# A gated attention layer whose prologue works by contraction steps: x, context and k's weight in pieces, q's weight ahead of v's, and batch 0's deviations by Ln, Exp and one Newton step

## The chip, the cores and the metric

The kernel runs on one core of one Trainium2 chip. The metric is device time in microseconds (us): of the kernel before, three runs gave 1958.17 to 1960.98 with a median of 1960.36. The engines are TensorE (PE; its weight loads are PEld), VectorE (DVE), ScalarE (ACT), GpSimd (POOL) and SyncE, whose queue (SPq) issues all transfers.

## What is computed

For 16 batches of 512 tokens with 512 channels, all float32: a gated cross-attention of the normalised x over a context, and a gated feed-forward of the result:

```python
m, v = mean(x), var(x); n = (x - m) / sqrt(v + 1e-5)        # layernorm, no weights
q = n @ Wq.T + bq;  k = ctx @ Wk.T + bk;  v = ctx @ Wv.T + bv    # 16 heads of 32
attn = softmax(mask_and_causal(q @ k.T * 32**-0.5)) @ v
x = x + tanh(g_xattn) * (attn @ Wo.T + bo)
y = layernorm(x); yp = y shifted by one token
r = sigmoid((mu_r*y + (1-mu_r)*yp) @ W_r.T);  kk = (mu_k*y + (1-mu_k)*yp) @ W_k.T
out = x + tanh(g_ffn) * r * (relu(kk)**2 @ W_v.T)
```

## The kernel before

Every engine's program is written out by hand and every engine runs its own in order; the engines meet at semaphores. One of 16 batches is a tile of 4 x 128 tokens by 4 x 128 channels. The channels are the contraction of the projections, so a projection of 128 output rows has four steps k = 0..3.

**Exact products.** A float32 operand is split in a high part (rounded to the matmul's fp32r, a CAST on ScalarE) and a low part (original minus high, a subtraction on VectorE). `exact_product` makes three 128x512 matmuls for each step k (L41 high by high, L42 and L43 the mixed ones). So each weight (wq, wk, wv, wo), the context c (kept transposed) and the transposed x all cost a ScalarE cast and a VectorE subtraction before TensorE can use them. `split_weights` (L642 on ScalarE, L1007 on VectorE) does that for a weight as a whole, 128x2048; for batch 0 the context is also done as a whole (L829, L1156).

**x.** VectorE takes statistics of four token blocks (L931, L938), GpSimd turns variance to 1/sqrt in `invert_deviations` (L470 to L486: an integer seed and three Newton steps, 16 dependent instructions), ScalarE applies it (`apply_layernorm`, L566), TensorE transposes each block with the identity (L1362, four 128x128), ScalarE casts (`high_part_x`, L573), VectorE subtracts (`low_part_x`, L942).

**q and k.** A projected group of four heads leaves its PSUM bank by ScalarE (high part, L582 for q, L591 for k), then VectorE (low part, L947, L953), and then by six DMAs that stack the parts into `q_stack` and `k_stack` (`stack_q`, `stack_k`, L305, L314), with rows for the mask, whose constant part GpSimd sets to 1.0 first (L532, `stacks_set`). v goes to SBUF by `copy_v` (L599).

**Slots.** After a prologue, 259 slots follow, one for each (batch, head): scores of head i (L1236), their row extrema by VectorE (L964), and for head i - 3 the probabilities (L1260), their exponent (L619), causal masking and partial sums on GpSimd (L440 to L457), every fourth slot the values (L1280 to L1290). The table `WORK` says which steps of the projections of this batch and the next lie in which slot. PSUM has two banks for projections and one for values; `BANK` and `BEFORE` say which tile uses which and whose reader must have ended (`free_bank`). From about 1340 us on the feed-forward follows.

**The prologue**, the part that the change touches, makes in this order on TensorE: k0 (four steps), x blocks 0 and 1, v0, x blocks 2 and 3, v1, q0, two steps of q1; then slot 0, whose scores wait for `q_stacked` and `k_stacked`. ScalarE begins with the gates (Tanh) and a table load for Exp and Ln:

```python
act.wait_ge(gate_loaded, 16)
act.wait_ge(pool_const, 5)
nc.scalar.copy(ident_parts[:], ident[:]).then_inc(ident_ready, 1)
nc.scalar.activation(gate[:], gate[:], ACT.Tanh).then_inc(gate_ready, 1)
```

SyncE's queue issues x as 1 MB, two gates, c, wk, wv, wq, bias columns, mu, mask, wo, bo (L292 and L396 to L410), and then waits for `mask_scaled`, stores the mask and stacks.

## Time and profile before

| | |
|---|---|
| median of 3 runs | 1960.36 us (1958.17 to 1960.98) |
| the profiled execution | 1958.57 us, its span 1956.8 us |
| granted TensorE clock, mean | 0.99 of 2.4 GHz |
| PE busy | 1898.7 us, 97% of the span |
| PEld busy | 1471.8 us, 75% |
| DVE busy | 1339.0 us, 68% |
| ACT busy | 1088.0 us, 56% |
| POOL busy | 1210.6 us, 62% |
| DMA moved | 229.66 MB, mean 117 GB/s |

The profile is of one execution. In the page's strip of 40 slices PE is busy at 4 tenths in the first slice and at 8 in the second, and at 9 in nearly all others. Busy time is of instructions in flight, so a PE that is busy throughout can still run at either level of its clock; the granted clock (PEclk) tells which.

### The profile page before, as it was taken

Reading aid. Unit: us, or ns where it says so; the run is one execution under the profiler, and the core shown is the slowest. Engines: PE = TensorE matmul, PEld = TensorE weight load, DVE = VectorE, ACT = ScalarE, POOL = GpSimd, SP = SyncE. Lnnn points to the kernel's source line nnn. Section 1 sums busy time; section 2 is a strip of 40 time slices with the busy share of each in tenths; the row PEclk is TensorE's granted clock in tenths of the full one; section 3 lists DMA queues with packets and bytes.
Section 4 is the critical chain, followed back from the end, with each engine's and each line's share of the span. In section 5 each row is a group of like instructions: output and inputs, shape, how many; then the busy total and the mean of one; then the engine's idle time right before and its main releaser. Section 6 shows DMA issues by size and latency. Waiting matters only on the chain.

```text
span 1956.8 us, 35230 instructions
## 1 busy us (share of the span) xinstructions
PE 1898.7 (97%) x11136; PEld 1471.8 (75%) x11136; DVE 1339.0 (68%) x3528; ACT 1088.0 (56%) x2059; POOL 1210.6 (62%) x2001
## 2 busy tenths in 40 slices
PE   4899999999999999999999999998989999999999
PEld 3677777777777777777777777776768888888887
DVE  4767767777676777777677677777566665756654
ACT  4555555555555555555555555555565666656562
POOL 4577767777777777767777677777633333434331
PEclk9999999999999999999999999998999999999999
DMA  6454554645545445554545446454223223232321
GB/s 190 104 126 117 140 128 108 163 109 126 126 122 156 118 121 122 136 147 104 143 117 137 122 114 164 112 139 122 72 102 108 87 91 104 75 108 76 108 65 65
DMA packets 128695, 229.66 MB, mean 117 GB/s; under 512 B 18656, under 2 KB 20704, under 8 KB 127616
## 3 DMA queue, kind: packets, MB, share of 16 engines
q1 hardware_dynamic: 128512, 227.43, 43.6%
q8 instruction: 90, 1.47, 0.3%
q14 instruction: 93, 0.76, 0.1%
HBM read 92.06 MB, written 33.59 MB: 64 GB/s over the span
## 4 chain that ended last, share of the span: by engine, by line
PE 75%; DVE 10%; POOL 6%; issue 5%; ACT 3%; DMA 1%; SPq 0%; ACTq 0%; POOLq 0%; DVEq 0%
PE proj_ps L41 12%; PE proj_ps L42 11%; PE proj_ps L43 11%; PE value_ps L1280 7%; PE score_ps L1236 6%; PE prob_ps L1260 5%; PE score_ps L41 3%; PE score_ps L42 3%; PE score_ps L43 3%; DVE score_ps L964 2%; PE sum_ps L1290 2%; DVE split_max L974 2%; PE sum_ps L43 1%; PE sum_ps L42 1%; PE value_ps L42 1%
## 5 line engine op out<-in xcount | busy, mean ns | idle before, releaser
L964 DVE CUSTOM_DVE_ANT_0 score_ps<-score_ps,causal 128x128 f32<-128x128 f32 (+3 forms) x1024 | 487.6, 505 | 284.6 <-PE score_ps L1236 282.9
L619 ACT ACTIVATE probs<-prob_ps 128x512 f32<-128x512 f32 (+1 forms) x768 | 394.3, 527 | 313.8 <-PE prob_ps L1260 179.1
L1236 PE MATMUL score_ps<-k_stack,q_stack 97*128 97x128 f32 (+3 forms) x1024 | 319.2, 353 | 9.0 <-DVE least L964 3.7
L1260 PE MATMUL prob_ps<-q_stack,k_stack 100*128 100x512 f32 (+3 forms) x1024 | 282.5, 317 | 6.1 <-ACT probs L619 4.6
L451 POOL TENSOR_TENSOR prob_sum<-probs 128x384 f32<-128x384 f32 x256 | 259.4, 1013 | 0.0
L1236 PEld LDWEIGHTS score_ps<-k_stack,q_stack 97*128 97x128 f32 x1024 | 188.6, 190 | 83.3 <-issue 30.7
L500 POOL TENSOR_TENSOR kact<-square,kact 128x512 fp32r<-128x512 f32 x64 | 83.9, 1322 | 235.3 <-ACT kact L695 235.3
L454 POOL TENSOR_TENSOR prob_sum<-prob_sum,probs 128x256 f32<-128x256 f32 x256 | 193.9, 758 | 37.3 <-POOL prob_sum L451 0.9
L1260 PEld LDWEIGHTS prob_ps<-q_stack,k_stack 100*128 100x128 f32 x1024 | 192.8, 192 | 28.9 <-issue 6.9
L440 POOL TENSOR_SCALAR_AFFINE_SELECT probs<-probs 128x256 f32<-128x256 f32 x256 | 104.8, 409 | 177.2 <-ACT probs L619 177.2
L444 POOL TENSOR_SCALAR_AFFINE_SELECT probs<-probs 128x256 f32<-128x256 f32 x256 | 106.9, 418 | 103.3 <-ACT probs L619 103.3
L1280 PE MATMUL value_ps<-probs,v 128*32 128x512 f32 (+3 forms) x2048 | 165.6, 442 | 0.1
L964 DVE DVE_READ_ACCUMULATOR2_ANT least<- 128x1 f32 x1024 | 144.4, 141 | 0.0
L1031 DVE TENSOR_TENSOR square<-square 128x512 f32<-128x512 f32 x64 | 45.5, 712 | 139.0 <-ACT square L687 138.9
L457 POOL TENSOR_TENSOR prob_sum<-prob_sum,probs 128x128 f32<-128x128 f32 x256 | 120.5, 471 | 20.1
L1020 DVE SCALAR_TENSOR_TENSOR tiles<-xT_room_high,mu,tiles 128x512 f32<-128x512 f32 x128 | 94.8, 760 | 49.5 <-ACT tiles L667 47.0
L41 PE MATMUL proj_ps<-cT_high,wk_high 128*128 128x512 f32 x256 | 102.4, 400 | 18.0 <-DVE wk_low L1007 18.0
L606 ACT COPY max_rows<-sum_ps 16x128 f32<-16x128 f32 x128 | 32.5, 254 | 152.8 <-PE sum_ps L1245 152.8
L41 PE MATMUL proj_ps<-mix_k_high,ffn_wk_high 128*128 128x512 f32 x256 | 104.3, 408 | 4.8 <-DVE mix_k_low L1026 3.6
L41 PE MATMUL proj_ps<-wo_high,attn_high 128*128 128x512 f32 x256 | 103.0, 402 | 2.1 <-DVE attn_low L995 1.3
L41 PE MATMUL proj_ps<-xT_high,wq_high 128*128 128x512 f32 x256 | 102.1, 399 | 1.6 <-DVE staged L947 1.6
L41 PE MATMUL proj_ps<-wv_high,cT_high 128*128 128x512 f32 x256 | 101.6, 397 | 1.0 <-DVE xT_low L942 1.0
(145 smaller groups left out, 4873.7 us busy)
## 6 DMA issues: line engine op xcount, KB each, us to landing
k_stack<-staged SPq DMA_DIRECT2D x384, 128.0 KB
q_stack<-staged SPq DMA_DIRECT2D x384, 128.0 KB, 3.1
tiles<-in_x SPq DMA_DIRECT2D x16, 1024.0 KB, 5.6
x_io<-in_x SPq DMA_DIRECT2D x16, 1024.0 KB, 7.9
x<-x_io SPq DMA_DIRECT2D x64, 256.0 KB, 3.1
res<-x SPq DMA_DIRECT2D x64, 256.0 KB, 3.7
out_x<-res SPq DMA_DIRECT2D x64, 256.0 KB, 2.0
tiles<-in_ctxT SPq DMA_DIRECT2D x60, 256.0 KB, 4.4
```

Source lines behind the costliest of these rows:

```text
L41: nc.tensor.matmul(out, s_high, m_high, start=first and n == steps[0], stop=False)
L42: nc.tensor.matmul(out, s_high, m_low, start=False, stop=False)
L43: done = nc.tensor.matmul(out, s_low, m_high, start=False, stop=last and n == steps[-1])
L444: nc.gpsimd.affine_select(out=pair, in_=pair, compare_op=ALU.is_ge, fill=0.0, base=0, pattern=[[0, 2], [1, P]], channel_multiplier=-1).the ...
L451: nc.gpsimd.tensor_tensor(total, here[:, P:S], here[:, PT_AT[1]:PT_AT[1] + LATE], ALU.add).then_inc(summed, 1)
L454: nc.gpsimd.tensor_tensor(total[:, P:LATE], total[:, P:LATE], here[:, PT_AT[2]:PT_AT[2] + 2 * P], ALU.add).then_inc(summed, 1)
L457: nc.gpsimd.tensor_tensor(total[:, 2 * P:LATE], total[:, 2 * P:LATE], here[:, PT_AT[3]:PT_AT[3] + P], ALU.add).then_inc(summed, 1)
L619: nc.scalar.activation(probs[:, u % RING, lo:hi], prob_ps[(3 * u + c) % 2][:, 0:hi - lo], ACT.Exp, scale=SCALE).then_inc(exp_done, 1)
L964: nc.vector.tensor_tensor_reduce(out=here, in0=here, in1=causal[:, LATE - P * t:S], scale=-1.0, scalar=3e38, op0=ALU.add, op1=ALU.min, acc ...
L1236: last = nc.tensor.matmul(here[:, at:at + P * (t + 1)], q_stack[n][0:MASK_ROW + 1, j, P * t:P * t + P], k_stack[n][0:MASK_ROW + 1, j, 0:P ...
L1260: last = nc.tensor.matmul(here[:, at:at + width], k_stack[n][0:ROWS, j, P * k:P * k + P], q_stack[n][0:ROWS, j, P * k:S], start=True, stop ...
L1280: nc.tensor.matmul(value_ps[DH * j:DH * j + DH, P * k:S], v[:, value_block(b, g), k, at:at + DH], probs[:, (HG * G + j) % RING, PT_AT[k]:P ...
```

## The change

It touches the first part of every engine's program. Transfers: the mask goes first, x comes as four blocks of 256 KB with a semaphore each, then c and wk by contraction step in turn (eight times 256 KB), then wq, wv, the columns, the mask's store, wo, and only then gates, mu and bo. ScalarE and VectorE split c and the four weights by step. Batch 0's deviations are made by Ln and Exp(-0.5 ln) on ScalarE and one Newton step of four small instructions on VectorE; GpSimd's 16 instructions for batch 0 go. GpSimd does the mask and the constant rows of the stacks at once, and the wait for those rows before the first scores is taken by TensorE. TensorE makes k0 in two halves with the transposes between and after them, then q0, then v0 and v1, and q1's two steps now wait for v0's copy. The Tanh of both gates stands behind the weights' casts on ScalarE, with a table load on either side of it. The diff, cut to its core:

```diff
-        FIRST = {"k0": None, "x0": None, "v0": ("x0", 0), "x2": ("v0", 0), "q1": ("q0", 0)}
+        FIRST = {"k0": None, "x0": None}
...
-            load_x(0)
+            sp.dma_start(x_io[0:B, 0, :].bitcast(I32), mask).then_inc(mask_loaded, 16)
+            for m in range(T):
+                sp.dma_start(tiles[:, m, :], x[0, P * m:P * m + P]).then_inc(x_first_loaded[m], 16)
+            for k in range(K):
+                sp.dma_start(c_raw[:, k, :], ctxT[0, P * k:P * k + P]).then_inc(c_first_loaded[k], 16)
+                sp.dma_start(w_raw["k"][:, k, :], wkT[:, k, :]).then_inc(wk_first_loaded[k], 16)
+            sp.dma_start(w_raw["q"], wqT).then_inc(w_loaded["q"], 16)
+            sp.dma_start(w_raw["v"], wvT).then_inc(w_loaded["v"], 16)
+            for n, col in enumerate((bq, bk, bv)):
+                sp.dma_start(columns[:, n, :], col).then_inc(columns_loaded, 16)
+            sp.wait_ge(mask_scaled, 1)
+            sp.dma_start(mask_bias, x_io[0:B, 1, :]).then_inc(mask_stored, 16)
+            sp.dma_start(w_raw["o"], woT).then_inc(w_loaded["o"], 16)
             sp.dma_start(gate[:], g_xattn.partition_broadcast(P)).then_inc(gate_loaded, 16)
             sp.dma_start(ffn_gate[:, 0:1], g_ffn.partition_broadcast(P)).then_inc(ffn_gate_loaded, 16)
-            sp.dma_start(c_raw, ctxT[0].rearrange("(k p) s -> p k s", p=P)).then_inc(c_raw_loaded, 16)
-            sp.dma_start(w_raw["k"], wkT).then_inc(w_loaded["k"], 16)
-            sp.dma_start(w_raw["v"], wvT).then_inc(w_loaded["v"], 16)
-            sp.dma_start(w_raw["q"], wqT).then_inc(w_loaded["q"], 16)
-            for n, col in enumerate((bq, bk, bv)):
-                sp.dma_start(columns[:, n, :], col).then_inc(columns_loaded, 16)
             for n, col in enumerate((mu_k, mu_r)):
                 sp.dma_start(mu[:, n, :], col).then_inc(mu_loaded, 16)
-            sp.dma_start(x_io[0:B, 0, :].bitcast(I32), mask).then_inc(mask_loaded, 16)
-            sp.dma_start(w_raw["o"], woT).then_inc(w_loaded["o"], 16)
             sp.dma_start(bo_gated[:], bo.partition_broadcast(P)).then_inc(bo_loaded, 16)
-            sp.wait_ge(mask_scaled, 1)
-            sp.dma_start(mask_bias, x_io[0:B, 1, :]).then_inc(mask_stored, 16)
...
-            invert_deviations(0)
-            pool.wait_ge(ln_step, NORM_STEPS)
-            for n, rows in enumerate(q_stack + k_stack):
-                nc.gpsimd.memset(rows[MASK_ROW:P].bitcast(F32), 1.0).then_inc(stacks_set, 1)
-                pool.wait_ge(stacks_set, n + 1)
...
             pool.wait_ge(mask_loaded, 16)
             nc.gpsimd.tensor_scalar(x_io[0:B, 1, :], x_io[0:B, 0, :].bitcast(I32), 0, MASKED, ALU.is_equal,
                                     ALU.mult).then_inc(mask_scaled, 1)
+            pool.wait_ge(pool_const, 5)
+            pool.wait_ge(mask_scaled, 1)
+            for n, rows in enumerate((k_stack[0], q_stack[0], k_stack[1], q_stack[1])):
+                nc.gpsimd.memset(rows[MASK_ROW:P].bitcast(F32), 1.0).then_inc(stacks_set, 1)
+                pool.wait_ge(stacks_set, n + 1)
...
+            def split_first_c(k):
+                act.wait_ge(c_first_loaded[k], 16)
+                nc.scalar.copy(cT[0][:, k, :], c_raw[:, k, :]).then_inc(c_high, 1)
+
+            def split_weights(name, k):
+                if name == "k":
+                    act.wait_ge(wk_first_loaded[k], 16)
+                else:
+                    act.wait_ge(w_loaded[name], 16)
+                nc.scalar.copy(w[name][0][:, k, :], w_raw[name][:, k, :]).then_inc(w_high[name], 1)
...
-            act.wait_ge(gate_loaded, 16)
+            nc.scalar.preload_act_table_set("natural_log_exp_and_others")
+            split_first_c(0)
+            act.wait_ge(variance_ready, 1)
+            nc.scalar.activation(newton[:, 1, :], newton[:, 2, :], ACT.Ln).then_inc(variance_logged, 1)
+            act.wait_ge(variance_logged, 1)
+            nc.scalar.activation(newton[:, 1, :], newton[:, 1, :], ACT.Exp, scale=-0.5).then_inc(seed_ready, 1)
...
             act.wait_ge(pool_const, 5)
             nc.scalar.copy(ident_parts[:], ident[:]).then_inc(ident_ready, 1)
+            act.wait_ge(gate_loaded, 16)
             nc.scalar.activation(gate[:], gate[:], ACT.Tanh).then_inc(gate_ready, 1)
             act.wait_ge(ffn_gate_loaded, 16)
             nc.scalar.activation(ffn_gate[:, 1:2], ffn_gate[:, 0:1], ACT.Tanh).then_inc(ffn_gate_tanh, 1)
             nc.scalar.preload_act_table_set("natural_log_exp_and_others")
...
-            dve.wait_ge(c_high, K)
-            nc.vector.tensor_tensor(cT[1][:], c_raw, cT[0][:].bitcast(F32), ALU.subtract).then_inc(c_low, K)
-            split_weights(0, "k")
-            split_weights(1, "v")
+            power, guess, variance, shift = (newton[:, n, :] for n in range(4))
+            dve.wait_ge(ln_stats, T)
+            nc.vector.tensor_scalar(variance, moments[:, :, 1], LN_EPS, None, ALU.add).then_inc(variance_ready, 1)
+            low_part_first_c(0)
+            dve.wait_ge(seed_ready, 1)
+            nc.vector.tensor_tensor(power, guess, guess, ALU.mult).then_inc(seed_step, 1)
+            dve.wait_ge(seed_step, 1)
+            nc.vector.scalar_tensor_tensor(out=power, in0=power, scalar=-0.5, in1=variance, op0=ALU.mult, op1=ALU.mult
+                                           ).then_inc(seed_step, 1)
+            dve.wait_ge(seed_step, 2)
+            nc.vector.scalar_tensor_tensor(out=guess, in0=power, scalar=1.5, in1=guess, op0=ALU.add, op1=ALU.mult
+                                           ).then_inc(seed_step, 1)
+            dve.wait_ge(seed_step, 3)
+            nc.vector.scalar_tensor_tensor(out=shift, in0=moments[:, :, 0], scalar=-1.0, in1=guess, op0=ALU.mult, op1=ALU.mult
+                                           ).then_inc(ln_step, NORM_STEPS)
+            split_weights("k", 0)
+            low_part_first_c(1)
+            split_weights("k", 1)
+            low_part_first_c(2)
+            split_weights("k", 2)
             low_part_x(0, 0)
-            low_part_x(0, 1)
+            low_part_first_c(3)
+            split_weights("k", 3)
+            for m in range(1, T):
+                low_part_x(0, m)
+            for k in range(K):
+                split_weights("q", k)
             low_part_k(0, 0)
-            split_weights(2, "q")
-            low_part_x(0, 2)
-            low_part_x(0, 3)
+            split_weights("v", 0)
+            split_weights("v", 1)
             low_part_q(0, 0)
+            split_weights("v", 2)
+            split_weights("v", 3)
...
+                if c == 0 and u in (0, HG):
+                    pe.wait_ge(stacks_set, (2, 4)[G])
...
-            pe.wait_ge(ident_ready, 1)
-            for k in range(K):
+            for k in range(2):
                 project_k(0, 0, k)
             transpose_x(0, 0)
             transpose_x(0, 1)
-            for k in range(K):
-                project_v(0, 0, k)
+            for k in range(2, K):
+                project_k(0, 0, k)
             transpose_x(0, 2)
             transpose_x(0, 3)
             for k in range(K):
-                project_v(0, 1, k)
-            for k in range(K):
                 project_q(0, 0, k)
+            for m in range(2):
+                for k in range(K):
+                    project_v(0, m, k)
+            pe.wait_ge(ident_ready, 1)
             for k in range(2):
```

On ScalarE, before: its first twelve instructions. `probs` is the room in which c, wk and wq arrive, `attn_room` that of wv and wo, `tiles` is x, `staged` are q's and k's parts on their way to the stacks.

```order
L823 ACT_TABLE_LOAD [waits pool_const]
L823 CAST ident_parts<-ident 128x128 [waits gate_loaded]
L824 ACTIVATE gate<-gate 128x1
L826 ACTIVATE ffn_gate<-ffn_gate 128x1 [waits ffn_gate_loaded]
L827 ACT_TABLE_LOAD
L829 CAST cT_high<-probs 128x2048 [waits c_raw_loaded]
L642 CAST wk_high<-probs 128x2048 [waits wk_loaded]
L566 ACTIVATE tiles<-tiles,newton 128x512 [waits ln_step] x4
L642 CAST wv_high<-attn_room_high 128x2048 [waits wv_loaded]
L573 CAST xT_high<-proj_ps 128x4x128 [waits xt_done]
L573 CAST xT_high<-value_ps 128x4x128 [waits xt_done]
L591 ACTIVATE staged<-proj_ps,columns 128x512 [waits k_done,columns_loaded]
```

And now, from the casts of wq to the copies of v:

```order
L654 CAST wq_high<-probs 128x512 [waits wq_loaded] x4
L596 ACTIVATE staged<-proj_ps,columns 128x512 [waits k_done,columns_loaded]
L654 CAST wv_high<-attn_room_high 128x512 [waits wv_loaded] x2
L587 ACTIVATE staged<-proj_ps,columns 128x512 [waits q_done]
L654 CAST wv_high<-attn_room_high 128x512 [waits wv_loaded] x2
L865 CAST ident_parts<-ident 128x128 [waits pool_const]
L867 ACT_TABLE_LOAD
L867 ACTIVATE gate<-gate 128x1 [waits gate_loaded]
L869 ACTIVATE ffn_gate<-ffn_gate 128x1 [waits ffn_gate_loaded]
L870 ACT_TABLE_LOAD
L604 COPY v<-proj_ps 128x2x256 [waits v_done] x2
```

The two table loads around Tanh stood ahead of all casts and now stand behind those of wq and wv, directly ahead of v's copies; q's high part (L587) now comes between v's casts.

On TensorE, before: from k0's last step to the first scores. A step of a projection is three rows and a transposed block two; here the first row of each stands, and of the steps that only repeat, none.

```order
L41 MATMUL proj_ps<-cT_high,wk_high 128x512 [waits w_low,c_low]
L1362 MATMUL proj_ps<-ident,tiles 128x128 [waits ln_applied]
L1362 MATMUL value_ps<-ident,tiles 128x128 [waits ln_applied]
L41 MATMUL proj_ps<-wv_high,cT_high 128x512 [waits w_low,c_low,xt_low]
...
L1362 MATMUL proj_ps<-ident,tiles 128x128 [waits ln_applied,v_copied]
L1362 MATMUL value_ps<-ident,tiles 128x128 [waits ln_applied,xt_low]
L41 MATMUL proj_ps<-wv_high,cT_high 128x512 [waits k_low]
...
L41 MATMUL proj_ps<-xT_high,wq_high 128x512 [waits w_low,xt_low]
...
L41 MATMUL proj_ps<-xT_high,wq_high 128x512 [waits q_low]
...
L1236 MATMUL score_ps<-k_stack,q_stack 128x128 [waits k_stacked0_0,q_stacked0_0]
```

And now, from k0's second step on:

```order
L41 MATMUL proj_ps<-cT_high,wk_high 128x512 [waits wk_low,c_low]
L1427 MATMUL proj_ps<-ident,tiles 128x128 [waits ln_applied]
L1427 MATMUL value_ps<-ident,tiles 128x128 [waits ln_applied]
L41 MATMUL proj_ps<-cT_high,wk_high 128x512 [waits wk_low,c_low]
...
L1427 MATMUL proj_ps<-ident,tiles 128x128 [waits ln_applied,xt_low]
L1427 MATMUL value_ps<-ident,tiles 128x128 [waits ln_applied,xt_low]
L41 MATMUL proj_ps<-xT_high,wq_high 128x512 [waits wq_low,xt_low]
...
L41 MATMUL proj_ps<-wv_high,cT_high 128x512 [waits wv_low,c_low,q_low]
...
L41 MATMUL proj_ps<-wv_high,cT_high 128x512 [waits k_low]
...
L41 MATMUL proj_ps<-xT_high,wq_high 128x512 [waits v_copied,ident_ready]
...
L1298 MATMUL score_ps<-k_stack,q_stack 128x128 [waits stacks_set,k_stacked0_0,q_stacked0_0]
```

q0 moved ahead of v0 and v1, so that 24 matmuls of v and six of q1 now stand between the end of q0 and the first scores, where six of q1 stood; q1 waits for v's copy and no longer for q0's low part.

## Rows read from the trace of the kernel before

**Rows 1.** Windows by stage: window, length, busy us of each engine, PEclk, DMA share, GB/s

```profile
18.00:40.70 22.70, 16.64 (x70) 12.65 (x70) 8.57 (x8) 10.51 (x12) 10.62 (x7) 1.00 0.40 106
40.70:48.50 7.80, 7.01 (x19) 5.59 (x20) 3.68 (x15) 0.69 (x1) 0.00 (x0) 0.56 0.83 205
48.50:100.00 51.50, 46.51 (x253) 33.15 (x256) 37.19 (x121) 26.36 (x53) 30.00 (x62) 0.90 0.51 109
100.00:1340.00 1240.00, 1231.85 (x7981) 932.54 (x7974) 906.80 (x2740) 681.38 (x1368) 923.72 (x1550) 1.00 0.52 128
```

**Rows 2.** Chain of waits, 0 to 50 us: start, us, what

```profile
2.79 10.81 DMA probs<-in_wkT
...
15.55 2.30 DVE wk_low L1007
17.99 0.77 PE proj_ps L41
...
25.98 0.23 PE proj_ps L41
...
34.65 0.70 ACT staged L582
...
36.15 0.57 SPq L305
...
44.66 0.43 PE proj_ps L41
```

**Rows 3.** Windows of the first transfers

```profile
5.50:7.00 1.50, 0.00 (x0) 0.00 (x0) 0.97 (x2) 0.00 (x0) 0.00 (x0) 1.00 0.04 2
...
8.50:11.00 2.50, 0.00 (x0) 0.00 (x0) 0.38 (x5) 1.27 (x1) 1.42 (x8) 1.00 1.09 435
```

**Rows 4.** Timeline 0 to 20 us: start, us, engine, line, operation [idle before <-releaser]

```profile
0.80 0.45 SPq L292 DMA_DIRECT2D tiles<-in_x  x1
...
6.03 2.47 DVE L931 BATCH_NORM_STATS2 stats<-tiles 128x6 f32<-128x512 f32 x4 [6.03 <-DMA tiles<-in_x]
...
7.14 0.30 ACT L823 CAST ident_parts<-ident 128x128 fp32r<-128x128 f32 x1 [3.55 <-DMA gate<-in_g_xattn]
7.35 0.20 ACT L824 ACTIVATE gate<-gate 128x1 f32<-128x1 f32 x1
...
8.49 1.28 ACT L827 ACT_TABLE_LOAD   x1
8.54 0.38 DVE L938 BATCH_NORM_AGGREGATE moments<-stats 128x2 f32<-128x6 f32 x4
...
11.19 1.90 ACT L829 CAST cT_high<-probs 128x2048 fp32r<-128x2048 f32 x1 [1.42 <-DMA probs<-in_ctxT]
...
15.61 2.93 ACT L566 ACTIVATE tiles<-tiles,newton 128x512 f32<-128x512 f32 x4
15.63 3.66 POOL L532 MEMSET q_stack<- 32x2048 f32 x2
```

**Rows 5.** Answers by source line: duration ns min/median/max, first and last start

```profile
L296 SPq DMA_DIRECT2D tiles<-in_ctxT x60: 327/442/2009, 92.9 to 1260.6; - x60
...
DMA to landing us min/median/max: 2.9/4.4/6.5
...
L612 ACT CAST cT_high<-tiles x60: 608/627/641, 95.9 to 1271.0; 128x512 fp32r<-128x512 f32 x60
L573 ACT CAST xT_high<-proj_ps x32: 557/585/589, 23.0 to 1259.7; 128x512 fp32r<-128x512 f32 x32
L974 DVE TENSOR_TENSOR split_max<-least,split_max x128: 166/169/1208, 49.7 to 1378.6; 128x8 fp32r<-128x8 f32 x128
```

**Rows 6.** Timeline of TensorE: the first scores and the first values

```profile
40.71 0.67 PE L1236 MATMUL score_ps<-k_stack,q_stack 97*128 97x128 f32 x3 [2.87 <-DMA q_stack<-staged]
...
76.97 1.06 PE L1280 MATMUL value_ps<-probs,v 128*32 128x512 f32 x8
```

**Rows 7.** Window of a later stretch at the lower clock

```profile
74.00:76.00 2.00, 2.00 (x7) 1.60 (x6) 1.59 (x4) 1.13 (x4) 1.86 (x4) 0.54 1.10 160
```

More of the change, by code:

```diff
@@ L147, in gated_layer @@
         sum_ps = psum("sum_ps")
-        w_loaded = {n: sem(f"w{n}_loaded") for n in "qkvo"}
-        w_high, w_low = sem("w_high"), sem("w_low")
+        w_loaded = {n: sem(f"w{n}_loaded") for n in "qvo"}
+        w_high, w_low = ({n: sem(f"w{n}_{part}") for n in "qkvo"} for part in ("high", "low"))
         ffn_loaded = {n: sem(f"ffn_w{n}_loaded") for n in "krv"}
@@ L162, in gated_layer @@
         xt_done, xt_high, xt_low = sem("xt_done"), sem("xt_high"), sem("xt_low")
-        c_raw_loaded = sem("c_raw_loaded")
+        variance_ready, variance_logged, seed_ready, seed_step = (sem(f"first_{n}") for n in ("variance", "logged", "seed", "step"))
+        x_first_loaded = [sem(f"x_first_loaded{m}") for m in range(T)]
+        c_first_loaded = [sem(f"c_first_loaded{k}") for k in range(K)]
+        wk_first_loaded = [sem(f"wk_first_loaded{k}") for k in range(K)]
         c_loaded = [sem(f"c_loaded{k}") for k in range(K)]
@@ L928, in layernorm_stats @@
             def layernorm_stats(b, m):
-                dve.wait_ge(x_loaded, 16 * (b + 1))
+                if b == 0:
+                    dve.wait_ge(x_first_loaded[m], 16)
+                else:
+                    dve.wait_ge(x_loaded, 16 * b)
                 wait(dve, ln_stats, T * b)
@@ L1117, in fourth @@
                     layernorm_stats(b + 1, 2)
[L1118 to L1119 removed]
+                if i in (1, 2):
+                    for k in range(2):
+                        split_weights("o", 2 * (i - 1) + k)
                 if i == N - 9:
@@ L1326, in project_v @@
                     pe.wait_ge(c_low, K * (b + 1))
-                    pe.wait_ge(w_low, 2)
+                if b == 0 and m == 0:
+                    pe.wait_ge(w_low["v"], k + 1)
                 last = exact_product(nc, bank(f"v{m}")[:], lambda k: [part[:, k, P * m:P * m + P] for part in cT],
@@ L1468, in _ @@
             pe.wait_ge(pool_const, 5)
-            pe.wait_ge(ident_ready, 1)
-            for k in range(K):
+            for k in range(2):
                 project_k(0, 0, k)
@@ L1478, in _ @@
             for k in range(K):
-                project_v(0, 1, k)
-            for k in range(K):
                 project_q(0, 0, k)
+            for m in range(2):
+                for k in range(K):
+                    project_v(0, m, k)
+            pe.wait_ge(ident_ready, 1)
             for k in range(2):
```

65 lines of the change are left out of this document (38 added, 27 removed).

## The prediction

> **What bounds the kernel now.** I read the stages first [rows 1]. From 100 to 1340 us TensorE is in flight for 1231.85 of 1240 us at full clock, and no edit is there. The change is about what comes before: TensorE's first matmul starts at 17.99 us [rows 2], from 18 to 40.7 us it is busy for 16.6 of 22.7, and only then do the 259 slots begin. Every later slot is placed relative to the first scores and not to the clock on the wall, so what counts is when slot 0 starts and how well the first slots run. Bounds of the rest (97% TensorE) don't move.
>
> The chain of waits [rows 2] names what sets 40.71 us. At its head one transfer, wk, in flight from 2.79 to 13.6 us; then its cast (until 15.55) and its subtraction (2.30), then the first matmul. At its tail: q0 has ended at 34.6, ScalarE's high part (0.70) and VectorE's low part last until 36.15, 1.5 us in all; there the DMAs for q's stack begin, and the first scores, which wait for them, start at 40.71 [rows 6]. So q is last, and 4.56 us pass between its first DMA and the scores. The windows of the transfers [rows 3] show that from 8.5 us on the queue moves 435 GB/s (0.60 us for 256 KB, 2.4 us for 1 MB) and that from 5.5 to 7.0 us it moves nothing, although c had been issued long before. The two gate DMAs lie between x and c there.
>
> **The change, step by step.**
>
> *Transfers.* x was issued at 0.80 us and VectorE could begin at 6.03 [rows 4]. A mask DMA of half a microsecond now stands ahead, so the last block of x lands at some 6.3 us, the first at 4.5. A 256 KB issue takes the queue 0.44 us [rows 5], less than the 0.60 us that its bytes need, so bytes set the pace. If the hole goes with the gates, c's first step lands at 6.9 and each of the seven pieces after it 0.62 us later: wk complete at 11.3 (before: 13.6), wq at 13.7, wv at 16.2. If the hole stays, all of these are 2 us later. I take that it goes, because c's bytes start only behind the gates' landing; the other end stays in the range. The Trainium skill ("DMA: Bandwidth & Descriptors", Rules for kernel authors) asks for at least 1 MiB per DMA for full bandwidth, which speaks against eight pieces of 256 KB. No row here shows pieces alone: the four of load_c land in 4.4 us in the middle [rows 5], beside stack DMAs.
>
> *Deviations.* Before, GpSimd's chain let the normalising start at 15.61 [rows 4]. Now: last statistics at 7.1, aggregation 0.38, one small VectorE instruction, Ln and Exp at about 0.2 each (Tanh of the gate took that [rows 4]), four small VectorE instructions at 0.17 to 0.21 each (one of that size stands in [rows 5]), plus the crossings: done at 9.0. First matmul: wk's first low part is behind that on VectorE, 0.7 us for a quarter of 2.30 and its fixed part, so about 9.8 instead of 17.99.
>
> *The new bound of the prologue is ScalarE, in order.* From c's first step (7.0) to the cast of wq's last step it has 12 casts (0.627 each alone, some 0.54 back to back [rows 5]) = 6.5; Ln and Exp 0.4; four normalisings 2.93 [rows 4]; four x casts of 0.585, overlapped 0.5 [rows 5] = 2.0; sum 11.8, so 18.8 without a wait. Waits I find when I lay the programs side by side: 1.2 us for the transpose of x block 0 (it stands behind two steps of k0, which run at the lower clock), 1 to 2 us for block 2, whose bank waits for VectorE's low part. wq's last cast then ends between 20.6 and 21.9, its subtraction 0.7 later, the step of q0 another 1 to 1.3 later. q0 ends at **24.1** (22.6 at best, 25.9 if TensorE is at 1.2 GHz throughout). Before: 34.6. Splitting a 2048-wide cast in four costs 4 x 0.54 against 1.90, 0.25 us each; that is in the sum.
>
> *q's low part.* 1.5 us as before, giving 25.6 instead of 36.12. VectorE has two subtractions of wv ahead of it, done by 24.7, so they hide. k's stack DMAs end at 26.2 (SyncE's queue, k's low part at 23.6 plus 1.9 and 0.7), so q's are issued at 26.2 and land at 30.8.
>
> *What is late next.* Between q0 and the scores TensorE now has v0, v1 and two steps of q1, 30 matmuls. v0 shares q0's bank and starts at 25.7. Pitch is 0.23 at full clock and 0.43 at half [rows 2]: 6.9 us at full, so 32.5; with all q0 and the first of v at half clock, 34.3. I take **33.3**. The DMAs (30.8) hide behind them. Before 40.71: gain **7.4** (8.2 to 6.4, and 2 less if the hole stays).
>
> *The clock in the first slots.* Before, TensorE had waited 2.87 us for q's stack [rows 6]; the granted clock then fell to half, mean 0.56 from 40.7 to 48.5 us [rows 1], the matmuls of a projection there at 0.43 pitch. A mean of 0.56 is 0.88 of 7.8 us, nearly 7, at half clock, of which some 6.4 in matmuls, worth up to 3.2. Now TensorE goes from q1 straight to the scores, so the cause is gone. VectorE's extrema and the stack DMAs hold part of it back: I take **2.2** (0 to 3.2).
>
> *Edits at nothing.* GpSimd's fills (3.66 for two [rows 4]) now end before 14 us and are wanted at 33; without that cover they would cost 7 us. The gate's wait (3.55 us [rows 4]) hid behind c, for which ScalarE waited another 1.42 us; going alone it would bring nothing. The Tanh group (0.3 + 1.28 + 0.4 + 1.28 = 3.3 us) now stands ahead of v0's copy, which q1's steps wait for: it ends at 29.1 to 29.7, and v1 keeps TensorE until 31.1. Gates landing: behind wo, at some 22, wanted at 27. wo's split: in idle ScalarE time of slot 0; VectorE takes it in two slots instead of one, which lets k1's low part through about 1 us earlier.
>
> One rule speaks against that group's new place. Both table loads show 1.28 us (one in [rows 4]), and what follows each in the trace waited for something else anyway, so no drain can be read. The Trainium skill ("ScalarE: Activation LUTs", What ACT_TABLE_LOAD costs) gives a drain of about 1.38 us with every switch.
>
> **Sum.** 7.4 + 2.2 = 9.6 us. The profiled execution took 1958.57 (span 1956.8 and 1.8 around it): 1949.0. It lies 1.8 below the median of the runs, near their lower end, so I put the new median at **1949.5**.
>
> **Rivals.**
>
> 1. *The hole stays or the pieces are slow.* For: 1.5 us without bytes [rows 3] may belong to the switch from x to c and not to the gates. Against: the queue never pauses between the other 1 MB loads. Price: c at 9.0, all of ScalarE's chain 2 us later, and matmuls at half clock: first scores 34.6 to 36.4, gain 4.3 to 6.1, plus up to 2.2 from the clock; about 1953.5. Chance 0.20.
> 2. *A table switch holds ScalarE longer than its 1.28 us*, by one more of the same length or so each. v0's copy then ends at 31.9 to 32.5, TensorE waits at q1 for some 1.3 us: 1950.8. By the skill's drain it would be the same within 0.2. Chance 0.07.
> 3. *More comes back.* The later drops to half clock (one is in [rows 7]) are what makes 0.90 of 48.5 to 100 us [rows 1]: 0.2 x 51.5 = 10 us at half clock, at 0.46 us each (1 - 0.23/0.43) some 4 us of matmuls; they follow short waits for GpSimd and x, and a differently paced start could miss them: 1945. Chance 0.07.
> 4. *No gain.* The dense start earns a new drop: 48.5 to 100 us already runs at 0.90 of the clock with 5 us of idle [rows 1]. Each microsecond at half clock costs 0.46. If the early slots spend some 17 us more at half clock, 8 of the 9.6 are gone: 1957.5. Chance 0.05.
> 5. *Slower.* The same at its end: TensorE, fed in small pieces by ScalarE, VectorE and GpSimd, doesn't get its full clock back in the ramp at all. Place: from 9.8 to 100 us. It decides when more than 21 us of added half clock have eaten the 9.6; 30 us would give 1963.2. For: [rows 7] show a drop that no long wait preceded. Against: from 100 us on the clock is full for 1240 us [rows 1], in the same loop. Chance 0.03.
>
> That the change doesn't do what it says (q0 ahead of v, pieces by step) is excluded by the order of the instructions.
>
> **How the numbers follow.** The forecast (gain 6 to 13) has 0.58, the rivals 0.20, 0.07, 0.07, 0.05, 0.03. A measurement can tell about 0.2%, 3.9 us, so faster means under 1956.4: all of the forecast, rivals 2 and 3 and most of 1, 0.89; the same 0.08; slower 0.03. The range takes the forecast's bounds and rival 1 in: 1944 to 1955.5.
>
> **What would show it.** First matmul at 9.8 us (17.99), normalising at 9 to 10 (15.61), bytes without a pause between x and c, q0's last matmul at 24 (34.6), q's first stack DMA at 26.2 (36.15), scores at 33.3 (40.71) released by TensorE's own q1 and not by a DMA, the windows after it at PEclk 1.00 where 0.50 stood, and 100 to 1340 us unchanged. The prediction is wrong if the scores start after 36, or if the ramp to the first values takes longer than before (76.97 - 40.71 = 36.3 us [rows 6]); then the gain went to the clock or to GpSimd's chain.

## The result, and the profile after it

| | before | after |
|---|---|---|
| median of 5 runs | 1958.56 us (1958.17 to 1960.98) | 1948.74 us (1946.63 to 1950.56) |
| ratio | | 0.9943, 95% interval 0.9932 to 0.9954 |
| the profiled execution, its span | 1958.57, 1956.8 us | 1947.00, 1945.0 us |
| first matmul, normalising | 17.99, 15.61 | 10.47, 10.70 |
| last matmul of q0 begins | 34.22 | 23.59 |
| first scores | 40.71 | 32.48 |
| first values | 76.97 | 65.61 |
| third values, and from there to the end | 119.34, 1837.5 | 107.64, 1837.4 |

The median of before is of the three runs that the prediction had and two more. The change is faster by 9.8 us between the medians, and by 11.6 between the two profiled executions. "First scores" is the start of slot 0's matmuls, "first values" and "third values" that of the first and third group of value matmuls. All of the gain is there by 108 us; what follows takes the same 1837 us. The windows by stage, the ones of [rows 1]:

```profile
18.00:40.70 22.70, 18.12 (x85) 14.43 (x83) 14.05 (x36) 14.17 (x25) 1.98 (x3) 1.00 0.68 168
40.70:48.50 7.80, 7.75 (x38) 6.31 (x38) 6.68 (x22) 3.02 (x6) 0.74 (x2) 1.00 0.66 141
48.50:100.00 51.50, 46.83 (x276) 33.62 (x276) 35.92 (x120) 29.94 (x61) 39.28 (x73) 0.90 0.45 95
100.00:1340.00 1240.00, 1231.71 (x7992) 931.32 (x7992) 905.06 (x2736) 682.80 (x1369) 920.60 (x1548) 1.00 0.52 130
```

From 40.7 to 48.5 us TensorE issues 38 matmuls at PEclk 1.00 where 19 ran at 0.56. Later nothing changed. PEclk doesn't tell everything, though: it reads 1.00 from the start, but the first 128x512 matmuls (10.47 to 15.72 us here, 17.99 to 20.69 before) take 0.63 us each and follow each other at 0.43, the pace of the lower level. The sums of half clock below leave that stretch out in every kernel.

The windows of the transfers, against [rows 3]: the stretch that moved 2 GB/s moves 374, but 8.5 to 11 us moves 316 where whole transfers moved 435.

```profile
5.50:7.00 1.50, 0.00 (x0) 0.00 (x0) 1.04 (x2) 0.00 (x0) 1.44 (x2) 1.00 0.98 374
...
8.50:11.00 2.50, 0.53 (x1) 0.50 (x2) 2.09 (x8) 2.18 (x6) 2.44 (x2) 1.00 0.97 316
```

The timeline of the start of the deviations (start, us, engine, line, operation), in the place of [rows 4]:

```profile
6.65 0.69 DVE L963 BATCH_NORM_STATS2 stats<-tiles 128x6 f32<-128x512 f32 x1 [0.22 <-DMA tiles<-in_x]
7.31 0.62 ACT L647 CAST cT_high<-probs 128x512 fp32r<-128x512 f32 x1 [5.24 <-DMA probs<-in_ctxT]
7.38 0.38 DVE L970 BATCH_NORM_AGGREGATE moments<-stats 128x2 f32<-128x6 f32 x4
7.80 0.59 DVE L1195 TENSOR_SCALAR newton<-moments 128x4 f32<-128x4 f32 x1
...
8.42 0.20 ACT L837 ACTIVATE newton<-newton 128x4 f32<-128x4 f32 x1 [0.49 <-DVE newton L1195]
...
10.47 0.76 PE L41 MATMUL proj_ps<-cT_high,wk_high 128*128 128x512 f32 x1 [10.47 <-DVE wk_low L1039]
```

The chain is the planned one, but for one row: L1195 adds epsilon to four elements per lane and takes 0.59 us, where other instructions of four elements take 0.16. Experiments 8 and 12 come back to it.

The chain of waits from q0's first matmul to the scores, in the place of the tail of [rows 2]: no DMA of q's stack is in it.

```profile
20.25 0.61 DVE wq_low L1039
21.00 0.47 PE proj_ps L41
23.75 0.24 PE proj_ps L43
24.02 0.70 ACT staged L587
24.74 0.76 DVE staged L979
25.54 0.50 PE proj_ps L41
32.64 0.25 PE score_ps L1298 x2
```

ScalarE's timeline around Tanh. Each instruction behind a table load begins as soon as the load's 1.28 us are over (25.95 + 1.28 = 27.23; 27.56 + 1.28 = 28.84).

```profile
25.95 1.28 ACT L867 ACT_TABLE_LOAD   x1
27.24 0.20 ACT L867 ACTIVATE gate<-gate 128x1 f32<-128x1 f32 x1
27.35 0.19 ACT L869 ACTIVATE ffn_gate<-ffn_gate 128x1 f32<-128x1 f32 x1
27.56 1.28 ACT L870 ACT_TABLE_LOAD   x1
28.85 0.59 ACT L604 COPY v<-proj_ps 128x512 f32<-128x512 f32 x1
```

### The profile page after: what moved, and what is told of

The parts are those of the page before. It is cut to its first block, busy times and chain, and to the rows that moved or that the text cites. A ratio compares the mean times of both kernels' runs of the same rounds, so it can differ in the third digit from the quotient of the medians.

```text
span 1945.0 us, 35215 instructions
## 1 busy us (share of the span) xinstructions
PE 1896.1 (97%) x11136; PEld 1470.8 (76%) x11136; DVE 1340.8 (69%) x3548; ACT 1091.4 (56%) x2077; POOL 1203.6 (62%) x1985
## 4 chain that ended last, share of the span: by engine, by line
PE 76%; DVE 10%; POOL 6%; issue 5%; ACT 3%; DMA 0%; ACTq 0%; SPq 0%; POOLq 0%; DVEq 0%
PE proj_ps L41 12%; PE proj_ps L42 11%; PE proj_ps L43 11%; PE value_ps L1342 7%; PE score_ps L1298 6%; PE prob_ps L1322 5%; PE score_ps L41 3%; PE score_ps L42 3%; PE score_ps L43 3%; DVE score_ps L996 2%; PE sum_ps L1352 2%; DVE split_max L1006 2%; PE sum_ps L42 1%; PE value_ps L42 1%; PE sum_ps L43 1%
```

## Experiments

Run 7 starts from the kernel before, 2 from run 1, 12 from run 8 and 10 is 8 and 9 together; every other is the changed kernel with one group of edits. A number in brackets behind one of a run is the changed kernel's, unless it says otherwise. What each kernel's profiled execution and its runs gave (us; half clock is TensorE's lower level, 1.2 instead of 2.4 GHz, summed over the windows of 2 us from 8 to 124 us with PEclk under 0.97, each its length by 2 x (1 - PEclk); the ratio is to the kernel before on the same chip):

| | first matmul | scores | scores to first values | third values | half clock | median | ratio, 95% interval |
|---|---|---|---|---|---|---|---|
| before | 17.99 | 40.71 | 36.26 | 119.34 | 17.0 | 1958.56 | 1 |
| after | 10.47 | 32.48 | 33.13 | 107.64 | 10.2 | 1948.74 | 0.9943 (0.9932, 0.9954) |
| 1 gates between | 12.75 | 36.34 | 33.08 | 111.66 | 13.5 | 1950.65 | 0.9959 (0.9944, 0.9974) |
| 2 gates, Tanh first | 14.29 | 37.83 | 33.58 | 113.60 | 17.0 | 1953.04 | 0.9966 (0.9953, 0.9979) |
| 3 GpSimd's chain | 10.13 | 39.02 | 32.75 | 111.73 | 17.1 | 1951.97 | 0.9969 (0.9957, 0.9982) |
| 4 v ahead | 12.32 | 38.96 | 35.26 | 114.55 | 13.7 | 1954.13 | 0.9973 (0.9962, 0.9984) |
| 5 whole transfers | 13.55 | 37.08 | 33.13 | 112.80 | 13.7 | 1950.44 | 0.9961 (0.9947, 0.9974) |
| 6 idle added | 10.57 | 37.86 | 35.48 | 117.23 | 17.0 | 1954.56 | 0.9980 (0.9970, 0.9990) |
| 7 order alone | 17.99 | 38.46 | 33.72 | 113.56 | 3.4 | 1955.30 | 0.9984 (0.9975, 0.9993) |
| 8 v in a third bank | 12.32 | 33.17 | 33.29 | 107.81 | 3.4 | 1946.54 | 0.9940 (0.9928, 0.9953) |
| 9 second batch too | 10.48 | 32.83 | 32.33 | 107.53 | 10.2 | 1950.88 | 0.9957 (0.9945, 0.9969) |
| 10 both | 10.48 | 32.81 | 32.25 | 107.30 | 13.6 | 1947.94 | 0.9948 (0.9936, 0.9960) |
| 11 changed, again | 10.46 | 34.13 | 33.15 | 109.52 | 13.5 | 1949.11 | 0.9951 (0.9938, 0.9964) |
| 12 fills later | 10.21 | 31.07 | 33.33 | 106.87 | 10.2 | 1947.09 | 0.9944 (0.9930, 0.9958) |

An interval is some 0.0024 wide, 4.7 us of the time, so the landmarks inside the traces tell more than the medians do.

**1.** The two gate DMAs back between x and c.

```diff
+            sp.dma_start(gate[:], g_xattn.partition_broadcast(P)).then_inc(gate_loaded, 16)
+            sp.dma_start(ffn_gate[:, 0:1], g_ffn.partition_broadcast(P)).then_inc(ffn_gate_loaded, 16)
             for k in range(K):
                 sp.dma_start(c_raw[:, k, :], ctxT[0, P * k:P * k + P]).then_inc(c_first_loaded[k], 16)
```

> The changed kernel, with the two gate transfers back between x and c. Theory (the gates made the hole of 1.5 to 2 us in the queue that the trace of before shows): c's first cast starts about 1.5 to 2 us later than 7.31 us, the first scores at about 34 to 34.5 instead of 32.48, the ramp after them as in the changed kernel (33.1 us to the first values), so about 1950.5 in all. Rival (the hole belongs to the switch from one large x transfer to c, and the pieces of x made it go): c's first cast within 0.5 us of 7.31, scores within 0.5 us of 32.48.

Its windows:

```profile
5.50:7.00 1.50, 0.00 (x0) 0.00 (x0) 0.11 (x1) 0.00 (x0) 1.44 (x2) 1.00 0.27 75
7.00:8.50 1.50, 0.00 (x0) 0.00 (x0) 1.16 (x2) 0.00 (x0) 1.44 (x2) 1.00 0.21 52
```

The hole is back: 3 us at a quarter of the DMA share. c's first cast begins at 9.92 (7.31), the first matmul 2.3 later. Rival 1 of the prediction is answered: the hole belonged to the gates. Its price is about what the prediction had put (2): the scores come 2.2 later than in run 11 (the changed kernel on another chip), whose clock went the same way: both run at half clock during q0, the first trace of the changed kernel doesn't, and so the expected 34 to 34.5 became 36.34.

**2.** Gates there and their Tanh ahead of c's first cast, as before.

> As the run before, and also the Tanh group (identity's copy, two Tanh, a table load on either side) back at the head of ScalarE's program, so that the stray wait for the gate is in again. Theory: with c in pieces the wait is no longer hidden: the Tanh group ends only after the second gate has landed (8 to 9 us) and another 1.5 us of Tanh and table load, so c's first cast starts at about 10 to 10.5 and the first scores at about 35 to 36; about 1952. It also shows what the group's place behind the casts was worth. Rival (ScalarE has slack before the scores): scores as in the run with the gates alone.

ScalarE waits for the gates until 9.33, loads its table at 10.16 and casts c at 11.45, 1.5 us after run 1; the scores come at 37.83, 1.5 after run 1's. So in the new prologue Tanh and its table load no longer hide ahead of c. Behind them, in the changed kernel, they do hide: v1 keeps TensorE until 31.1.

**3.** Batch 0's deviations by GpSimd's 16 instructions, the fills behind them.

```diff
-            nc.vector.tensor_scalar(variance, moments[:, :, 1], LN_EPS, None, ALU.add).then_inc(variance_ready, 1)
...
+            invert_deviations(0)
+            pool.wait_ge(ln_step, NORM_STEPS)
```

> The changed kernel with batch 0's deviations by GpSimd's 16 instructions again (behind the mask's scaling, ahead of the fills), no Ln and Exp, no Newton step on VectorE. Theory: the chain takes 6.6 us as before instead of 2.0, so the normalising starts at about 14.3 instead of 10.70, everything behind it on ScalarE moves by 3 to 3.6 us, and the first scores start at about 35.5 to 36; about 1952. The first matmul comes a little earlier than 10.47 (VectorE is free of the four small instructions). Rival (casts of c and wk set the order anyway): scores under 33.5.

Normalising starts at 14.32 (10.70) and the scores come at 39.02, 6.5 later, more than the chain is longer and more than the 3 to 3.5 expected: TensorE begins k0 at 10.13, waits 1.73 and 1.27 us, and runs at half clock from 16 to 31 us. The early start of TensorE is worth nothing when the next input isn't there. Of the 6.1 us of GpSimd's chain, some 1.6 are four of its small instructions that took 0.47 to 0.73 us instead of 0.2 beside VectorE's subtractions; the section on the hardware comes back to that.

**4.** v's weight and projections ahead of q's, with everything else of the change.

```diff
-            sp.dma_start(w_raw["q"], wqT).then_inc(w_loaded["q"], 16)
             sp.dma_start(w_raw["v"], wvT).then_inc(w_loaded["v"], 16)
+            sp.dma_start(w_raw["q"], wqT).then_inc(w_loaded["q"], 16)
```

> The changed kernel with v ahead of q again on all engines and in the transfers, all else in pieces. Theory: q0 then ends at about 29.5 and its low part at 31, the stack DMAs and their 4.6 us are in the open: first scores at about 35.5, after an idle TensorE of 2.5 to 3 us, and the granted clock drops to half after it as in the kernel before, so the ramp to the first values takes about 36 us instead of 33.1: values at 71.5, about 1954.5 in all. Rival (the drop in the clock was chance and not the idle time): scores at 35.5, but the ramp stays at 33 us, 1951.5.

ScalarE's copies of v and the part of q0 stand ahead of the Tanh group here. The old wait is there again, 2.81 us against the 2.87 of [rows 6], and a drop with it, of 3.4 us at half clock where before had 6.8:

```profile
38.96 0.67 PE L1294 MATMUL score_ps<-k_stack,q_stack 97*128 97x128 f32 x3 [2.81 <-DMA q_stack<-staged]
```

```profile
40.00:42.00 2.00, 1.60 (x4) 1.31 (x5) 1.62 (x6) 0.00 (x0) 0.00 (x0) 0.63 0.96 172
42.00:44.00 2.00, 2.00 (x7) 1.61 (x7) 0.74 (x4) 0.00 (x0) 0.00 (x0) 0.51 0.88 212
```

Of the 6.5 us by which its scores are late, 1.85 have the cause of run 12, and an early drop like run 11's takes another 1.65. The rest, some 3, is the order. Its 2.1 us of longer way to the first values aren't the wait's alone: a later drop, from 66 to 75 us, is 6.8 us long where the changed kernel's is 3.4.

**5.** x, c and wk whole, one DMA each.

> The changed kernel with x, c and wk as one transfer of 1 MB each (engines still work by step). Theory (what pieces give is that the first step can start before the last has landed): x's statistics start at about 6.3 instead of 4.0 and end 1.3 us later than now, c's first cast at about 9 instead of 7.31, wk's at 11.5 instead of 8.77; the first matmul at 13 instead of 10.47 and the first scores 2 to 2.5 us later than 32.48; about 1951. Rival (the pieces cost bandwidth, so that whole transfers end earlier and make up for it): wk complete before 10.5 us, scores within 1 us of 32.48.

Its window of the transfers:

```profile
8.50:11.00 2.50, 0.00 (x0) 0.00 (x0) 2.40 (x8) 1.03 (x3) 2.44 (x2) 1.00 1.05 437
```

437 GB/s where the pieces of the changed kernel move 316 (and those of run 1 388), yet c's first cast is at 9.56 (7.31), wk's at 12.06 (8.77), the scores 3.0 later than in run 11. The Trainium skill ("DMA: Bandwidth & Descriptors", Rules for kernel authors) asks for 1 MiB or more per DMA: the bandwidth of that window points the same way, the time doesn't, since the first piece is wanted and not the last.

**6.** The changed kernel, and the first scores held until GpSimd has done eleven more small fills.

```diff
+            for n in range(11):
+                pool.wait_ge(held, n) if n else None
+                nc.gpsimd.memset(inverse[:], 1.0).then_inc(held, 1)
...
+                if c == 0 and u == 0:
+                    pe.wait_ge(held, 11)
```

> The changed kernel with one wait added: TensorE's first scores also wait for GpSimd to have filled an unused tile eleven times, until about 35.6 us, 3 us of idle TensorE. Theory (the idle before the scores is what made the clock fall and stretched the ramp by 3.1 us in the kernel before): scores at 35.6, granted clock 0.50 for about 6 us after it, values at about 71.5 to 72 (ramp 36 instead of 33.1): 6 us later in all for 3 us of wait; about 1954.5. Rival (the ramp is shorter because of wo's split, the earlier table and so on): clock stays 1.00 or its fall costs nothing, values at 68.7, about 1951.5.

This is the clock term by itself: no transfer, order or size is touched. TensorE stands 3.56 us, and its next 8 us run at 0.57:

```profile
38.00:46.00 8.00, 7.22 (x21) 5.65 (x22) 4.06 (x16) 0.69 (x1) 0.00 (x0) 0.57 0.07 24
```

From the scores to the first values it takes 35.48 us, and 33.15 in run 11: 2.3 us.

**7.** The kernel before, with nothing of the change but q ahead of v (transfer, casts, projections).

> The kernel before with one part alone: q ahead of v, in the transfers, on ScalarE, VectorE and TensorE, all in whole weights, gates first, deviations on GpSimd. Theory (the order hides the stack DMAs under v's 24 matmuls and keeps the clock up): first matmul at 18.0 as before, q's low part at about 31.5, scores at about 38 to 38.5 released by TensorE's own work, ramp 33 to 33.5 us without the drop: gain of about 5.5 us, half of the whole, about 1953. Rival (the gain came from the pieces alone): scores at 40 or later, the drop as before, gain under 2 us.

The scores come 2.25 earlier, TensorE doesn't stand before them, and the window of [rows 1] with 0.56 is at full clock:

```profile
40.70:48.50 7.80, 6.75 (x33) 5.40 (x32) 6.76 (x20) 1.64 (x3) 0.00 (x0) 1.00 0.52 160
```

It gains 0.16% (0.07 to 0.25%), about 3 us, where 5.5 were expected. The third values of its trace do come 5.8 us earlier than before's, but by the medians only half of that is left at the end; where it goes stays open. By the medians the order alone is near a third of the change.

**8.** v0 in the bank of the values, so that it needn't wait for q0's low part, and v1 behind q1's first steps. The third cast and subtraction of wv also go ahead of q's parts.

```diff
+        def v_bank(b, m):
+            return value_ps if b == 0 and m == 0 else bank(f"v{m}")
```

> The changed kernel with v0 of batch 0 in the values' PSUM bank, q1's two steps ahead of v1, and the third cast and subtraction of wv ahead of q's parts. Theory: TensorE no longer waits 1.56 us for q0's low part ahead of v0, and q1 no longer for v0's copy; the scores are then bound by the stack DMAs (30.8) or TensorE (31.3): at about 31.3 instead of 32.48, 1.1 us less in all, about 1947.6. Rival (q's low part comes later because of the third subtraction, and its DMAs with it): scores at 32 or later.

The wait of 1.56 us before v0 is gone (v0 follows q0 at 25.90), but the scores come at 33.17 and not at 31.3, because the first matmul is 1.85 late. The timeline of VectorE has it in one row:

```profile
8.38 1.86 DVE L1198 TENSOR_SCALAR newton<-moments 128x4 f32<-128x4 f32 x1
```

and GpSimd's:

```profile
6.55 1.80 POOL L543 MEMSET q_stack<- 32x2048 f32 x1
8.41 1.80 POOL L543 MEMSET k_stack<- 32x2048 f32 x1
10.27 1.80 POOL L543 MEMSET q_stack<- 32x2048 f32 x1
```

**9.** Batch 1's deviations by Ln, Exp and one step as well, because in the changed kernel GpSimd's chain ends at 58.96 and TensorE stands 1.36 us at 59. **10.** 8 and 9 together.

> The changed kernel, with batch 1's deviations made in the same way (Ln and Exp on ScalarE in slot 5, the rest on VectorE) instead of GpSimd's 16 instructions there. Theory: in slot 5 ScalarE stood 1.26 us for GpSimd's chain (54.5 to 59.0 us), with it TensorE 1.4 us, and the granted clock fell to half from 60 to 64 us; all of that goes, and the first values, which waited for GpSimd's sums, come 3 to 4 us earlier (62 instead of 65.6): about 1945. Rival (GpSimd's time is needed anyway, or the clock falls elsewhere): values less than 1.5 us earlier, total within 1.5 us of 1948.7.

> The two improvements together (v0 in the third bank with q1 ahead of v1; batch 1's deviations without GpSimd). Theory: they add up: scores at 31.3, values at about 61, 1944. Rival: the second takes the clock's drops away by itself and the first then brings nothing beyond its 1.1 us at the scores, or the sum is lost in a later drop (78 to 88 us): 1946.

From the scores to the first values they take 32.33 and 32.25 us, 0.8 less, so the chain did cost that. But half clock comes at 60 us all the same, and both traces have a wait late in the program that the changed kernel's lacks:

```profile
1317.79 1.07 PE L1359 MATMUL value_ps<-probs,v 128*32 128x512 f32 x8 [1.85 <-POOL prob_sum L462]
```

By the medians 9 gained nothing and 10 can't be told from the changed kernel. Why the late wait appears stays open.

**11.** The changed kernel again, on the chip of 9 and 10.

> The changed kernel itself, on the same chip as the two runs with it, as their yardstick. Its five runs were spread from 1946.6 to 1950.6; every theory expects a median of 1948.7 within 1.5 us, scores at 32.5 and values at 65.6.

0.9951 beside 0.9943, within the intervals. But the trace isn't the same: q0 begins at 21.03 after the same wait of 2.25 us, and this time its matmuls run at half clock from 22 to 25 us:

```profile
22.00:24.00 2.00, 2.00 (x6) 1.51 (x6) 2.00 (x5) 1.14 (x3) 0.00 (x0) 0.50 0.00 0
```

In the first trace that window was at 1.00. The scores are 1.65 us later, and so is all that follows. So one kernel, after the same wait of 2.25 us, drops or doesn't. One thing differs ahead of that wait. In the first trace:

```profile
15.72 0.63 PE L43 MATMUL proj_ps<-cT_high,wk_low 128*128 128x512 f32 x1
16.91 0.48 PE L41 MATMUL proj_ps<-cT_high,wk_high 128*128 128x512 f32 x1 [0.56 <-DVE wk_low L1039]
```

and in run 11:

```profile
15.47 0.40 PE L43 MATMUL proj_ps<-cT_high,wk_low 128*128 128x512 f32 x1
16.97 0.47 PE L41 MATMUL proj_ps<-cT_high,wk_high 128*128 128x512 f32 x1 [1.10 <-DVE wk_low L1039]
```

In run 11 TensorE reached the higher level sooner (the matmul takes 0.40 us and not 0.63). So k0's third step ended sooner, and TensorE stood longer before the fourth, whose input came at nearly the same time. The section on the hardware sets this beside the other runs.

**12.** Run 8 with the four fills behind the deviations.

```diff
             pool.wait_ge(mask_scaled, 1)
+            pool.wait_ge(ln_step, NORM_STEPS)
             for n, rows in enumerate((k_stack[0], q_stack[0], k_stack[1], q_stack[1])):
```

> The run e8_v_in_third_bank with one wait more: GpSimd begins its four fills of constant rows (1.80 us each, 4.70 to 12.07 us so far) only when batch 0's deviations are done. In nine traces so far the small TENSOR_SCALAR of VectorE that opens the chain (variance plus epsilon, 4 elements wide) took 0.30 to 1.86 us, and in all of them it ended 0.02 to 0.04 us before GpSimd's next fill began: 8.39 and 8.41 in the changed kernel, 10.24 and 10.27 in e8. Theory (a lock between the two engines): with no fill in the air it takes 0.2 us or less whenever it starts, the chain ends 1.9 us earlier than in e8, the first matmul comes at 10.0 to 10.6 (12.32 in e8), the first scores at 31.0 to 31.7 (33.17), and the median falls by 1 to 2.2 us from e8's 1946.54, to 1944.3 to 1945.5. The fills then end near 17 us and are wanted at 31. Rival (the instruction is slow by itself or behind the transfers that land at that time): it still takes 0.3 to 1.9 us, the first matmul stays at 10.5 to 12.3, and the time within 0.5 of e8's. Second rival (the fills now hold up other instructions of VectorE, between 9.5 and 17 us): subtractions of 0.69 us grow there and the scores stay near 33.

```profile
7.77 0.17 DVE L1199 TENSOR_SCALAR newton<-moments 128x4 f32<-128x4 f32 x1
7.97 0.20 ACT L841 ACTIVATE newton<-newton 128x4 f32<-128x4 f32 x1
...
9.61 1.80 POOL L544 MEMSET k_stack<- 32x2048 f32 x1 [5.04 <-DVE newton L1210]
```

The 4-element instruction takes 0.17 us, the first matmul comes at 10.21 (12.32 in run 8) and the scores at 31.07 (33.17), all as the lock has it; no subtraction grew. The median missed the 1944.3 to 1945.5 expected: 1947.09, with an interval that overlaps those of 8 and of the changed kernel. By the third values 0.9 is left of the 2.1 us, and from 72 to 92 us run 8 ran at PEclk 1.00, this one at 0.83.

```profile
72.00:92.00 20.00, 18.02 (x113) 11.42 (x113) 13.64 (x42) 11.56 (x25) 13.50 (x20) 0.83 0.54 133
```

Runs 8 and 12 are the lowest medians, but neither is shown to be faster than the changed kernel.

## Why the prediction was right

1948.74 was measured, 1949.5 predicted, inside 1944 to 1955.5. In the profiled execution the two terms came out larger than their sizes, 8.2 and 3.1 us for 7.4 and 2.2, and its 1947.00 is 2.0 below the 1949.0 of the sum. That execution was a lucky one: run 11's trace of the same kernel, at 1948.92, has a drop more. So the mechanism was right, and that the median fits within 0.8 us is in part luck.

- *Transfers.* The hole went with the gates; run 1 brings both back. Last block of x 6.65 for 6.3, c's first step 7.3 for 6.9. That bytes would flow at 0.62 us per piece was too good: 311 to 316 GB/s from 7 to 11 us, 0.8 us per 256 KB. It cost little, because ScalarE was the bound by then.
- *Deviations.* Done at 9.72 for 9.0: 0.35 from x, and 0.4 from L1195. First matmul 10.47 for 9.8. The step that failed is "GpSimd's fills ... at nothing": they hid from TensorE as said, but not from VectorE. In this trace it was cheap; in 4 and 8 the same instruction took 1.66 and 1.86 us and the first matmul moved by 1.85 (in 1 and 2 its 1.2 and 1.4 us hid behind c). The reading of before was off as well. GpSimd's chain ended at 15.57, but ScalarE had the cast of wk ahead of the normalising until 15.52 (13.62 and 1.90 us, shown below), so the chain alone didn't set the 15.61. It was the new order on ScalarE that gave the shorter chain its worth, and run 3 measures that: 3.6 us of the normalising.
- *ScalarE as the new bound.* wq's last cast ended at 21.5 (20.6 to 21.9), q0 at 24.0 (24.1), its low part at 25.5 (25.6), q's stack DMAs from 26.18 (26.2). The sum of casts in order came from rows of before alone, and it put the casts right. Two things in it are loose. Its waits, 1.2 and 1 to 2 us on 18.8, give 21.0 to 22.0 for wq's last cast where the prediction wrote 20.6 to 21.9. And the last cast isn't what set q0's end: its subtraction was over at 22.66 and TensorE took its step at 23.14 without a wait. What set it was q0's first step at 21.00, behind the subtractions of x's last blocks and of wq's first step, and then its own 12 matmuls at 0.23 us. Both ways end between 23 and 24 us, so that number is partly luck.
- *Scores.* 32.48 for 33.3, the early end of 32.5 to 34.3: gain 8.2, not 7.4. The mis-sized term is the clock for q0 and the first of v, which was taken as part half and ran full: 30 matmuls in 6.9 us. Run 11 shows the other outcome, 34.13. Both ends of that range were real.
- *The clock in the first slots.* 2.2 predicted; the ramp to the first values shrank from 36.26 to 33.13, 3.1, the upper end. This term was taken too small. Before's drop has 6.8 us of half clock, at the prediction's 0.46 each 3.1. Run 6 puts 6.8 us of half clock back by an added wait alone and measures 2.3 (run 4's 2.1 has a longer later drop in it); the rest isn't told apart.
- *Nothing-cost edits.* The gate's wait: that going alone it would have brought nothing before is read from before's trace and was not run. Runs 1 and 2 show that, left ahead of c in the new prologue, gates and Tanh would have cost 3.7 us of the scores (37.83 against run 11's 34.13), 2.2 of it the hole. Tanh's group: hidden, v0's copy ends at 29.4.
- *Rivals.* 1 is out (run 1). 2 is out: no instruction behind a load waited longer than 1.28 us. The Trainium skill ("ScalarE: Activation LUTs", What ACT_TABLE_LOAD costs) gives a drain of about 1.38 us with every switch; neither load here shows it. 3: the later half clock stayed at 10.2 us (before: 17.0 in all, 6.8 of it ahead of 60 us), so nothing more came back. 4 and 5: no half clock was added here, 3.3 us were in run 11 and 13.7 in run 3, so the mechanism exists, and is what the spread of the medians' runs (1946.63 to 1950.56) would look like; that it makes that spread was not tried.

## What to carry to other kernels

In a prologue, sum the in-order work of the engine that feeds all others, and put last what can run while the last transfer lands; that order alone gave 3 of the 10 us. A wait just before a dense stretch can cost twice, its own length and the half clock behind it (3.56 us of waiting cost 2.3 more in run 6). Work called free because its engine is idle must be held against what its neighbour does meanwhile.
